# Dense steps of the next layer at the end of a layer, passes that end with a chunk, and copies signalled by halves

## The reference, cut to what matters

```
for l in 0, 1, 2:
    msg  = relu(x @ pW[l] + pb[l])[src]                  # one row of 256 for each edge
    agg  = segment_sum(msg, dst, 6250)
    out  = (agg / max(degree, 1)) @ lW[l] + lb[l] + x @ rW[l]
    x    = silu(out / |out|)         # layers 0 and 1; layer 2: out / |out|, then layernorm, then + x1
```

## Time and profile before

| | us |
|---|---|
| median of 3 runs (2974.45 to 2976.66) | 2975.55 |
| the profiled execution | 2972.55 |
| its span | 2970.7 |
| PE busy | 2640.5 (89%) |
| DVE busy | 2221.8 (75%) |
| POOL busy | 1985.5 (67%) |
| ACT busy | 1676.1 (56%) |
| first gather of layer 0 starts | 1245.8 |
| first gather of layer 1 starts | 1820.4 |
| first gather of layer 2 starts | 2397.1 |

### The profile page before, as it was taken

The page is one execution under the profiler, slowest core; times in us unless marked ns, Lnnn a source line. Parts: engine busy times, 40 slices in busy tenths (PEclk is TensorE's granted clock), DMA queues, the critical chain, the costliest instruction groups (busy, mean ns, idle before and its releaser), DMA issues.

```text
span 2970.7 us, 49107 instructions
## 1 busy us (share of the span) xinstructions
PE 2640.5 (89%) x13426; PEld 1859.5 (63%) x13426; DVE 2221.8 (75%) x7629; ACT 1676.1 (56%) x3730; POOL 1985.5 (67%) x2041
## 2 busy tenths in 40 slices
PE   7699999999999899789999998899999988888884
PEld 5477777777677677466666665566666556655552
DVE  6369999999999999556666666566666647877885
ACT  5357777778777787355554553455555434434430
POOL 3576777767667776177776665777766657777772
PEclk9699999999999999799999999999999999999995
DMA  8767787777777777377776655777666567777762
GB/s 231 216 197 211 225 237 229 230 230 229 228 225 222 229 231 231 119 232 228 224 220 198 209 172 170 227 219 230 214 204 197 151 202 229 247 245 239 234 211 67
DMA packets 455093, 630.37 MB, mean 212 GB/s; under 512 B 94496, under 2 KB 373088, under 8 KB 454816
## 3 DMA queue, kind: packets, MB, share of 16 engines
q0 software_dynamic: 97184, 280.55, 33.4%
q1 hardware_dynamic: 325568, 301.63, 32.7%
q10 hardware_dynamic: 32064, 44.98, 4.2%
HBM read 551.28 MB, written 75.63 MB: 211 GB/s over the span
## 4 chain that ended last, share of the span: by engine, by line
PE 43%; DVE 36%; issue 7%; POOL 6%; ACT 3%; DMA 2%; DVEq 0%; SPq 0%; POOLq 0%; ACTq 0%
PE ps L1303 21%; DVE cell_marks L2090 6%; DVE ring L2019 6%; PE ps L1355 5%; PE ps L1377 4%; DVE lane_marks L2091 4%; POOL ring L1248 4%; PE ps L1341 4%; PE ps L1315 3%; DVE block_cube L804 2%; POOL ring L621 2%; PE ps L1881 2%; DVE block_ey L1993 2%; DVE block_inv_norm L806 2%; DVE attention_work L1996 2%
## 5 line engine op out<-in xcount | busy, mean ns | idle before, releaser
L1248 POOL DMA_INDIRECT ring<-message_table,src_index x1209 | 1181.6, 977 | 556.3 <-issue 379.7
L621 POOL DMA_INDIRECT ring<-attention_table,src_index x784 | 777.7, 992 | 308.0 <-issue 225.0
L1303 PE MATMUL ps<-count_rows,high_rows 128*128 128x512 f32 x1764 | 756.5, 429 | 99.7 <-ACT attention_work L1635 71.4
L1303 PE MATMUL ps<-count_rows,low_rows 128*128 128x512 f32 x1764 | 717.4, 407 | 0.0
L1645 ACT ACTIVATE count_rows<-one_hot 128x512 fp32r<-128x512 uint8 x882 | 524.6, 624 | 182.7 <-PE ps L1303 171.4
L1303 PEld LDWEIGHTS ps<-count_rows,high_rows 128*128 128x128 f32 x1764 | 345.2, 196 | 213.5 <-issue 92.8
L1881 PE MATMUL ps<-ring,one_hot 128*128 128x265 f32 x1568 | 438.6, 404 | 2.2 <-issue 2.1
L1524 DVE CAST high_rows<-attention_work 128x512 fp32r<-128x512 f32 x441 | 194.4, 441 | 287.1 <-PE ps L1303 267.8
L1303 PEld LDWEIGHTS ps<-count_rows,low_rows 128*128 128x128 f32 x1764 | 345.8, 196 | 74.5
L1881 PEld LDWEIGHTS ps<-ring,one_hot 128*128 128x128 f32 x1568 | 304.7, 201 | 63.5 <-issue 8.2
L1526 DVE TENSOR_TENSOR low_rows<-attention_work,high_rows 128x512 fp32r<-128x512 f32 x441 | 309.9, 703 | 15.2
(11 more groups left out here) (199 smaller groups left out, 3624.1 us busy)
## 6 DMA issues: line engine op xcount, KB each, us to landing
attention_work<-message_table SPq DMA_DIRECT2D x432, 256.0 KB
one_hot<-dense_adjacency SPq DMA_DIRECT2D x126, 448.0 KB, 4.2
attention_work<-in_dst_edges SPq DMA_DIRECT2D x112, 448.0 KB
ring<-message_table,src_index POOLq DMA_INDIRECT x1209
dense_adjacency<-root ACTq DMA_DIRECT2D x24, 784.0 KB, 6.1
attention_sums<-sums_out SPq DMA_DIRECT2D x112, 132.5 KB
ring<-attention_table,src_index POOLq DMA_INDIRECT x784
message_table<-attention_work ACTq DMA_DIRECT2D x98, 128.0 KB, 2.9
```

The lines of the kernel that those rows point to most:

```text
L621: pool.indirect_dma_start(m.ring[:, k, t, 0:cols], None, table, bass.IndirectOffsetOnAxis(ap=m.src[:, at:at + 1], axis=0)).then_inc(s[f"ro ...
L1248: pool.indirect_dma_start(m.quad_ring[:, k, j, :], None, m.tables[w.l], bass.IndirectOffsetOnAxis(ap=m.src[:, t:t + 1], axis=0)).then_inc( ...
L1303: last = nc.tensor.matmul(m.ps[:, 2 + half, 0:cols], rows[:, v % SPLITS, half * P:(half + 1) * P], m.a_rows[:, k, 0:cols], start=(j == 0 a ...
```

## The change: what it does

There are four parts, in layers alone.

1. **A table for each layer.** A class `Order` makes `steps_done`, `taken`, `order` and `combine_after` for its layer.
2. **Dense steps of the next layer.** In chunks 44 to 50 of layers 0 and 1 five steps of the next layer's first pass stand in each chunk (5, 10, 15, 20, 25, 30, 34 by the end of the chunks), and 2 more after the combine of slot 48: 36 in all. Layers 1 and 2 begin with 36 steps done and 6 more ahead of chunk 0. The source blocks of their first pass come in the order in which the layer before writes them, in bunches of 7 (bunches 0, 4, 1, 5, 2, 3, 6). SP waits for a message block's own write rather than for the whole table, and DVE splits only rows of blocks written by then (`written`).
3. **Passes that end with a chunk.** Layer 0 ends its passes with chunks 6, 13, 21, 28, 36 and 43; layers 1 and 2 with chunks 0, 9, 17, 26, 34 and 43. The steps of a chunk are spread evenly within a pass: about 6.5 for a chunk in layer 0, 5.7 in layers 1 and 2.
4. **Halves.** `turned` counts each of the two copies; a step's matmuls into a bank wait for that bank's copy alone. ACT's casts up to the pass's end are put ahead of the copies.

```diff
@@ the numbers
-DENSE_EARLY = 6
-ROWS = STEPS + STEPS % 2
-DENSE_LAST = 43
+ROWS = STEPS
+DENSE_LAST = 44
+AHEAD_RATE = 5
+AHEAD_LATE = 3
+FIRST_STEPS = 6
@@ class Order
+    def __init__(self, l, before):
+        self.l, self.final, self.before = l, l == LAYERS - 1, before
+        self.ahead = [0] * WORK
+        self.early = (before.begun if before else 0) + FIRST_STEPS
...
+    def steps_done(self, q):
+        if q >= DENSE_LAST:
+            return STEPS + self.ahead[q]
+        chunk, steps = -1, self.early
+        for part in range(PASSES):
+            end = self.pass_end(part)
+            if q <= end:
+                return steps + ((part + 1) * BLOCKS - steps) * (q - chunk) // (end - chunk)
+            chunk, steps = end, (part + 1) * BLOCKS
+
+    def pass_end(self, part):
+        steps, left = (part + 1) * BLOCKS - self.early, STEPS - self.early
+        return (2 * steps * DENSE_LAST + left) // (2 * left) - 1
...
+    def begin_next(self):
...
+        for q in range(DENSE_LAST, WORK):
+            self.ahead[q] = min(AHEAD_RATE * (q - DENSE_LAST + 1), self.written(blocks, q))
+        self.blocks_next = blocks
+        self.begun = min(self.ahead[-1] + AHEAD_LATE, self.written(blocks, WORK))
+
+    def written(self, blocks, q):
+        first = sum(map(len, self.taken[:q - 1]))
+        rows = [d for d, n in enumerate(blocks) if self.order.index(n) > first - 3]
+        return rows[0] // 2 * 2
...
@@ sync, stream
             for at, j, rows in pair_runs(v // 2):
+                if w.l and d < BLOCKS:
+                    at_slot = max(ORDERS[w.l - 1].order.index(n) for n in range(j, j + rows))
+                    for parity in range(2):
+                        sp.wait_ge(s[f"put{parity}"], 16 * ((BLOCKS * (w.l - 1) + at_slot + 2 - parity) // 2))
...
-            table_done(sp, w.l)
@@ tensor
-            if j == 0:
-                pe.wait_ge(s["turned"].sem, s["turned"].free(w.pass0 + d // BLOCKS))
             for half in range(2):
+                if j == 0:
+                    pe.wait_ge(s["turned"].sem, s["turned"].free(2 * (w.pass0 + d // BLOCKS) + half))
...
-            done = 0
-            while done < DENSE_EARLY:
+            done = sweeps[w.l - 1].plan.begun if w.l else 0
+            while done < w.plan.early:
...
+            def node_late(i):
+                nonlocal done
+                second(w, i)
+                if i == BLOCKS - 1 and not w.final:
+                    while done < STEPS + w.plan.begun:
+                        sweep_step(w, done)
+                        done += 1
@@ scalar
             for k in range(2):
-                last = nc.scalar.activation(m.agg_t[:, k, 0:cols], m.ps[:, 2 + k, 0:cols], ACT.Copy)
-            last.then_inc(s["turned"].sem, 1)
+                nc.scalar.activation(m.agg_t[:, k, 0:cols], m.ps[:, 2 + k, 0:cols], ACT.Copy).then_inc(s["turned"].sem, 1)
...
-                if turns < PASSES and steps_done(q) >= (turns + 1) * BLOCKS:
+                if turns < PASSES and w.plan.steps_done(q) >= (turns + 1) * BLOCKS:
+                    while ready < w.step0 + (turns + 1) * BLOCKS:
+                        cast(ready)
+                        ready += 1
                     turn(w, turns)
                     turns += 1
```

More of the change, by code:

```diff
@@ L1075, in part_of @@
     return max(part for part in range(PASSES) if PASS_AT[part] <= col)
[L1078 to L1107, removed]
@@ L1121 @@
+ORDERS = []
+for layer in range(LAYERS):
+    ORDERS.append(Order(layer, ORDERS[-1] if ORDERS else None))
+assert all(sorted(made.order) == list(range(BLOCKS)) for made in ORDERS)
 class Sweep:
     def __init__(self, l):
-        self.l, self.final = l, l == LAYERS - 1
+        self.l, self.final, self.plan = l, l == LAYERS - 1, ORDERS[l]
         self.chunk0 = l * WORK
@@ L1131, in block @@
     def block(self, i):
-        return ORDER[i]
+        return self.plan.order[i]
     def slots_at(self, q):
-        return [ORDER.index(n) for n in TAKEN[q]]
+        return [self.plan.order.index(n) for n in self.plan.taken[q]]
     def there(self, i):
@@ L1140, in dense @@
     def dense(self, i):
-        return ORDER[i] < DENSE_BLOCKS
+        return self.plan.order[i] < DENSE_BLOCKS
     def walk(self, chunk, first, second):
@@ L1180, in pair_runs @@
 def pair_runs(x):
[L1183 to L1187, removed]
+    l, d = divmod(2 * x, ROWS)
+    first, second = ORDERS[l].block_at(d), ORDERS[l].block_at(d + 1)
+    return [(0, first, 2)] if second == first + 1 else [(0, first, 1), (1, second, 1)]
 def rows_of(x):
@@ L1294, in sweep_step @@
         def sweep_step(w, d):
+            if d >= STEPS:
+                w, d = sweeps[w.l + 1], d - STEPS
             u = w.step0 + d
@@ L1415, in late @@
                 turn(w, i - 1)
-            w.walk(chunk, late, lambda i: second(w, i))
+            def node_late(i):
[5 more added lines that the diff above has]
+                        done += 1
+            w.walk(chunk, late, node_late)
     @block.vector
@@ L1450, in merge @@
             if leaving >= DENSE_BLOCKS:
-                dve.wait_ge(s["lmm"].sem, s["lmm"].done(w.slot0 + ORDER.index(leaving)))
+                dve.wait_ge(s["lmm"].sem, s["lmm"].done(w.slot0 + w.plan.order.index(leaving)))
             elif w.l:
@@ L1532, in _, with split_to, chunk @@
             put_at(w, 0)
-            def chunk(q):
+            def split_to(rows):
                 nonlocal pairs
-                while 2 * pairs + 2 <= min(w.row0 + (steps_done(q - 1) if q else 0) + SPLITS, w.row0 + ROWS):
+                while 2 * pairs + 2 <= rows:
                     split(pairs)
                     pairs += 1
+            def chunk(q):
+                split_to(w.row0 + w.plan.rows_ready(q, w.plan.steps_done(q - 1) if q else w.plan.early - FIRST_STEPS))
                 if q + 1 < WORK:
@@ L1546, in chunk @@
                     first(w, i)
-                    while 2 * pairs + 2 <= min(w.row0 + combine_after(q, k) + SPLITS, w.row0 + ROWS):
-                        split(pairs)
-                        pairs += 1
+                    split_to(w.row0 + w.plan.rows_ready(q, w.plan.combine_after(q, k)))
                     second(w, i)
@@ L1555, in late, with node_late @@
                 first(w, i)
-            w.walk(chunk, late, lambda i: second(w, i))
+            def node_late(i):
+                second(w, i)
+                if i == BLOCKS - 1 and not w.final:
+                    split_to(w.row0 + w.plan.rows_ready(WORK, STEPS + w.plan.begun))
+            w.walk(chunk, late, node_late)
     @block.scalar
@@ L1629, in turn @@
             act.wait_ge(s["streamed"].sem, s["streamed"].done(w.step0 + (part + 1) * BLOCKS - 1))
-            used = w.slot0 + (ORDER.index(PASS_AT[part] // P - 1) if part else ORDER.index(DENSE_BLOCKS - 1) - BLOCKS)
+            used = w.slot0 + (w.plan.order.index(PASS_AT[part] // P - 1) if part else ORDERS[w.l - 1].order.index(DENSE_BLOCKS - 1) - BLOCKS)
             if used >= 0:
```

64 lines of the change are left out of this document (45 added, 19 removed).

## The result

The changed kernel takes 2903.93 us (median of 6 runs, 2900.42 to 2905.66) against 2976.11 (6 runs, 2971.43 to 2979.49): ratio 0.9757, 95% interval 0.9744 to 0.9769. The forecast was 2906. The profiled execution of the change took 2900.42 us, its span is 2898.6, and the first gathers of the three layers start at 1236.9, 1814.4 and 2357.6 us.

What follows compares the result with a forecast made beforehand. PE bounds layers 0 and 1, with POOL's gather issue just below; layer 2 was near POOL's floor. Layers: -0.9 - 37.4 - 31.0 = -69.3 on a 2970.7 span, 2901.4, as a median 2906 us; range 2880 to 2952.

Steps and rivals of the forecast that it cites:

- a pass end: PE's wait on ACT's copies (4.3 us) and the slow clock behind it (2.1) go: 6.4 us each, five a layer.
- the lighter start: Layer 0's early chunks carry 6.5 rather than 6.7 steps; PE waits on gathers and pays 3 steps later: +2.8 us.
- steps ahead, layer 0: 36 steps of layer 1 add 33.6 us to layer 0, less 5.3 of slot-chain waits they fill: +28.3.
- the late two steps: Two steps behind slot 48's combine lie in PE's 1.92 us gap before the last transposes, costing nothing.
- the extra split: DVE's extra split pair (1.1 us) ahead of slot 47's evacuation costs nothing; if uncovered, 1.1 us for each of two layers.
- walk of the chunks: Layer 1, chunk by chunk: 508.4 us of PE's work plus 18.7 of gather waits, 527.1 to the last sums.
- about 35 us: Sign at the program's end: time behind the last gather falls to about 35 us instead of 50.
- The wait that stays (1): Pass-end waits stay in part, 2 us plus the slow 2.1 at each end: +40, 2946 us; chance 0.10.
- the low clock (3): Clock falls in chunks waiting for POOL, every second one in layers 1 and 2: +53, 2959 us; chance 0.08.
- the slow rows (5): Chunks 44 to 50, layers 0 and 1: dense steps wait for late rows, 6.8 us a pair: 3151 us; chance 0.06.
- Rival 2: Layer 2's merge, combine and finish chain sets its chunk; it gains 10 rather than 31 us: 2927; chance 0.12.
- Rival 4: POOL is no floor; gathers speed up with PE, layer 1's 18.7 us of waits go: 2844 us; chance 0.04.

Runs made afterwards that it cites:

- mid_chunk: The change with passes ending in the middle of a chunk again, steps ahead and halves kept: 2946.92 us, 0.9915 of the kernel before.
- no_ahead: The change without its steps ahead (rate 0, late 0), passes still ending with a chunk and halves signalled: 2886.13 us, 0.9714 of the kernel before.
- no_ahead_43: no_ahead with the dense steps done by chunk 42 instead of 43: 2870.42 us, 0.9653 of the kernel before.

## Why the prediction was right, point by point

| step | forecast | measured |
|---|---|---|
| a pass end | -6.4 | -6.4 by mid_chunk in layer 0; -5.5 by no_ahead, with the lighter start in it; -7.2 by no_ahead_43, without it |
| the lighter start, layer 0 | +2.8 | +8.6 (no_ahead against no_ahead_43, one execution each) |
| steps ahead, layer 0 | +28.3 | +28.3 |
| layer 0 | 573.7 | 577.5, 576.1 |
| layer 1 | 539.3 | 543.2, 541.0 |
| layer 2 | 542.6 | 541.0, 541.0 |
| change of the three | -69.3 | -66.8 (means of two) |
| median | 2906 | 2903.9 |

*Pass ends.* Right in place and reason: PE's waits on the copies went from 71.4 us in the three layers (21.5, 21.5 and 28.4) to 1.0 (2.9 in the second execution), by what now stands between and not by a faster ACT. The size was right by one measure of three. Halves: worth nothing, as said.

*Layer 0.* The sum was right within 4 us, with some luck in it. Its terms without the steps ahead, -32 and +2.8, make -29.2, and -27.3 was measured; but both sizes were too small, as no_ahead_43 has -35.9 for the pass ends and no_ahead adds 8.6 for the lighter start. The step that "the late two steps lie in that same gap" for nothing failed: they wait for their rows' split, which DVE reaches only behind the slot's inverse root. That the extra split is "nothing" failed with it, since PE waits for it at 1806.00. Up to the end of the last sums layer 0 takes 562.0 and 562.1 us in the change's two executions, where the forecast had 573.7 - 12.2 = 561.5; all that is over lies behind them, 15.5 and 14.0 us against 12.2.

*Layer 1.* The walk of the chunks came out almost exactly: the last sums end 527.2 and 526.5 us behind the first gather, 527.1 were forecast. Its 18.7 us of gather waits were 14.6 (and 2.0 for a split at the layer's start, which the walk had not), and its parts as written add up to 507.4 rather than 508.4, so part of the match is luck. The mis-sized term is the end: 12.2 us from the last sums to the next first gather were taken from layer 0, where the clock had stayed up, while layer 1 of the same trace has 2397.10 - 2383.75 = 13.4. In the change it is 16.0 and 14.5, with the late steps, and this is all of the 3.9 and 1.7 us that layer 1 came out over. Chunks with five steps in the tail of layer 0 were to take 9.4 us; the flips of the change at 1753.63, 1763.06, 1772.50 and 1781.92 are 9.43 apart.

*Layer 2.* Right, 1.6 us too high. POOL's waits for PE add up to 2.4 us (8.4 before), and PE's waits for gathers to 68.8.

*The medians.* The forecast was 2 us too high in the end although the three layers brought 2.5 less than forecast; the attention block, which varies by 10 us, hides both. So it is in part luck that the median came within 2 us.

*What the prediction didn't ask.* It added a +28.3 in layer 0 to gains in layers 1 and 2 that it ascribed to fewer steps and to pass ends together, and never asked what each gives alone. Its own numbers answer that: without steps ahead layer 1 has the same floor (514.6 + 4.8 + 12.2 = 532 by POOL) and PE has the same work in it. The second part of the change (the steps ahead) is a loss of 16 us that the third part (the pass ends) covers.

*Signs.* Chunks in the middle of layer 1 follow each other by 10.2 to 10.3 us, and POOL's waits for PE have nearly gone (41.1 to 1.5 us in layer 1, 8.4 to 2.4 in layer 2), both as said. The "about 35 us" behind the program's last gather did not agree with the forecast's own sum, which leaves 542.6 - 514.6 = 28.0; 26.4 were measured. Dense steps waited on `low_rows` at the late steps and at the start of a layer, but nowhere in chunks 44 to 50.

*Rivals.* The wait that stays (1), the low clock (3) and the slow rows (5) are out: copies 1.0 us; granted clock 0.98 and 0.99 in layers 0 and 1, and in layer 2 0.89, where it was 0.90 and the gathers set the time; and no wait for rows in chunks 44 to 50. Rival 2 is out by layer 2's 26.4 us behind its last gather. Rival 4 is out by the gathers, which take 513 us or more from first to last in every layer of every kernel that makes all 403.

The Trainium skill (Perfetto Trace Analysis, Identifying the Most-Contended Engine) takes GpSimd's occupancy for its headroom. Here the measurement decides against it: POOL is 73% busy in layer 2 of the change and bounds it, with 0.30 us between gathers that no semaphore explains.

## What to carry to other kernels

Put between two halves of a handover (a bank's last write, its evacuation, its next first write) work of the same engine that needs neither; that took away 70 us of waits here, and splitting the signal as well added nothing. Before moving work from one stage to another, find the floor of both: work moved out of a stage that another engine already bounds comes back as waiting, while the stage that receives it pays (28.3 us here, with 12 returned). Where two bounds lie within a per cent, when a stage's light and heavy parts fall matters as much as its sum, and one number of the schedule (43 or 44) was worth about as much as leaving out the whole second part of the change (15.7 and 17.8 us by the medians).

## What the runs showed of the hardware that was not expected

The same two gaps on PE, 1.9 us before slot 48's transposes and then 0.5, left the clock up at one place and not at the other, within one execution. The kernel before, at the end of layer 0 (eight matmuls in 1.99 us) and of layer 1 (3.50 us for the same eight):

```profile
1815.42 0.44 PE L698 MATMUL ps<-ident,block_h 128*128 128x128 f32 x2 [1.92 <-ACT block_h L1616]
1816.34 1.99 PE L1355 MATMUL ps<-w_pr,block_hT 128*128 128x256 f32 x8 [0.47 <-ACT block_hT L1575]
2391.01 0.44 PE L698 MATMUL ps<-ident,block_h 128*128 128x128 f32 x2 [1.92 <-ACT block_h L1616]
2391.93 3.50 PE L1355 MATMUL ps<-w_pr,block_hT 128*128 128x256 f32 x8 [0.47 <-ACT block_hT L1575]
```

The two transposes take 0.44 us in both, so their length says nothing of the clock that the next matmuls get. The prediction took "after 1.85 us of waiting the clock had not fallen" from just that length, in one row.

The gap of 2.44 us ahead of the late steps did both as well. In the first execution of the change it lowered the clock in both layers (eight matmuls in 3.5 us, from 1806.00 and from 2348.70); in the second it left the clock up in both (2.0 us):

```profile
1814.24 0.51 PE L1355 MATMUL ps<-count_rows,high_rows 128*128 128x512 f32 x1 [2.44 <-DVE low_rows L1586]
```

So a gap of about 2 us may cost its 1.5 us or not, and two executions of one kernel can differ by that.
